# The first 512 rows' gated products moved into the rounds of the stage before, in a six-stage decoder kernel

## The reference

```python
x = _layernorm(x + _L0_attn_ref(x, ...))          # stage A: causal attention with a conv on v
x = _layernorm(x + _L0_xattn_ref(x, ctx_768, ...))  # stage B: cosine of Wv x and Wt ctx, 256 x 256, added to x
x = _layernorm(x + _L0_ffn_ref(x, ...))           # stage C: ternary feed-forward, below
x = _layernorm(x + _L1_attn_ref(x, ...))          # stage D: linear attention
x = _layernorm(x + _L1_xattn_ref(x, ctx_768, ...))  # stage E: cross attention
x = _layernorm(x + _L1_ffn_ref(x, ...))           # stage F: 8 experts, top 2
```

```python
def _L0_xattn_ref(visual_features, text_features, Wv, bv, Wt, bt):
    v = einsum('bsd,hd->bsh', visual_features, Wv) + bv
    t = einsum('bsd,hd->bsh', text_features, Wt) + bt
    dots = einsum('bih,bjh->bij', v, t)
    vn, tn = norm(v, axis=-1), norm(t, axis=-1)
    return dots / maximum(vn[:, :, None] * tn[:, None, :], EPS)
def _L0_ffn_ref(x, w1_w, w1_s, w2_w, w2_s, h1_w, h1_s, h2_w, h2_s, w3_w, w3_s):
    h = silu(_tlin(x, w1_w, w1_s)) * _tlin(x, w2_w, w2_s)   # 256 -> 1024, "gated products"
    h = gelu(_tlin(h, h1_w, h1_s))                          # 1024 -> 1024
    h = gelu(_tlin(h, h2_w, h2_s))
    return _tlin(h, w3_w, w3_s)                             # 1024 -> 256
```

## Time and profile before

| what | value |
|---|---|
| median of 3 runs | 1569.43 us (1557.24, 1571.11, 1569.43) |
| profiled execution, its own time | 1566.94 us |
| its span, first to last instruction | 1564.9 us |
| PE busy | 1326.4 us, 85% of the span |
| DVE, POOL, ACT busy | 1075.8, 800.9, 570.1 us |
| stages A and B, up to the last xt_lo | about 156.5 us |

### The profile page before, as it was taken

How to read it: one execution, slowest core, us unless ns; L and a number is a source line. 1 busy time by engine, 2 the same in 40 slices (tenths; PEclk the granted TensorE clock), 3 DMA queues, 4 the chain that set the end, 5 groups by cost and what they waited for, 6 DMA issues and landing times.

```text
span 1564.9 us, 23343 instructions
## 1 busy us (share of the span) xinstructions
PE 1326.4 (85%) x9071; PEld 1118.8 (71%) x9071; DVE 1075.8 (69%) x1729; ACT 570.1 (36%) x1171; POOL 800.9 (51%) x762
## 2 busy tenths in 40 slices
PE   6996999999989989977798989896582798989890
PEld 6985788778868868855566766665452798989890
DVE  4655766766676676543777677677673688888886
ACT  3666211211111021123344444443330565666552
POOL 4343666656656566523222433534443776767652
PEclk9997999999999999999999999998685899999995
DMA  5100333233223233212233215323400855555525
GB/s 167 37 21 1 111 94 115 81 92 98 81 81 99 76 94 94 61 39 56 94 99 120 82 40 120 88 58 95 115 8 25 293 211 192 209 191 207 192 71 161
DMA packets 58044, 163.23 MB, mean 104 GB/s; under 512 B 10598, under 2 KB 26185, under 8 KB 50000
## 3 DMA queue, kind: packets, MB, share of 16 engines
q1 hardware_dynamic: 45760, 100.13, 22.2%
q0 software_dynamic: 12176, 61.63, 11.1%
HBM read 136.47 MB, written 27.08 MB: 105 GB/s over the span
## 4 chain that ended last, share of the span: by engine, by line
PE 60%; DVE 17%; issue 7%; DMA 6%; ACT 5%; SPq 3%; POOL 2%; ACTq 0%; POOLq 0%; DVEq 0%
PE bank L388 13%; PE bank L390 13%; PE bank L389 13%; PE bank L1210 9%; PE bank L396 4%; SPq L717 3%; DVE topE L1714 2%; DVE hid_hi L1589 2%; DMA split_qk<-qk_lo 2%; PE bank L1052 2%; DVE shiftE L1723 2%; DMA xt_hi<-split_qk 2%; DVE hf L1605 2%; PE bank L1039 1%; PE bank L1128 1%
## 5 line engine op out<-in xcount | busy, mean ns | idle before, releaser
L520 POOL TENSOR_TENSOR wpiece_lo<-wraw,wpiece_hi 128x1024 fp32r<-128x1024 f32 x88 | 216.9, 2464 | 7.4
L1591 DVE TENSOR_TENSOR hid_lo<-hf,hid_hi 128x512 fp32r<-128x512 f32 x96 | 213.8, 2227 | 3.3
L388 PE MATMUL bank<-hid_hi,wpiece_lo 128*128 128x512 f32 x512 | 202.4, 395 | 12.9 <-DVE hid_lo L1591 12.9
L390 PE MATMUL bank<-hid_hi,wpiece_hi 128*128 128x512 f32 x512 | 200.7, 392 | 0.0
L389 PE MATMUL bank<-hid_lo,wpiece_hi 128*128 128x512 f32 x512 | 200.7, 392 | 0.0
L518 POOL TENSOR_SCALAR wpiece_hi<-wraw 128x1024 fp32r<-128x1024 f32 x88 | 95.0, 1080 | 186.2 <-PE bank L390 182.3
L1589 DVE CAST hid_hi<-hf 128x512 fp32r<-128x512 f32 x96 | 79.6, 830 | 125.7 <-ACT hf L1326 124.6
L1326 ACT ACTIVATE hf<-bank,ffn_scales 128x512 f32<-128x512 f32 x64 | 44.2, 690 | 293.8 <-PE bank L390 293.8
L636 POOL TENSOR_SCALAR staging<-staging 128x1024 f32<-128x1024 f32 x64 | 66.7, 1041 | 138.9 <-ACT staging L1411 138.6
L1210 PE MATMUL bank<-w_hi,gh_lo 128*128 128x256 f32 x368 | 106.1, 288 | 22.5 <-issue 21.8
L388 PEld LDWEIGHTS bank<-hid_hi,wpiece_lo 128*128 128x128 f32 x512 | 96.8, 189 | 39.1 <-DVE hid_lo L1591 19.3
(11 more groups left out here) (337 smaller groups left out, 3711.4 us busy)
## 6 DMA issues: line engine op xcount, KB each, us to landing
wraw<-in_C_w SPq DMA_DIRECT2D x88, 512.0 KB, 3.6
split_qk<-qk_hi SPq DMA_DIRECT2D x64, 128.0 KB, 2.4
split_qk<-qk_lo SPq DMA_DIRECT2D x64, 128.0 KB, 2.4
xt_lo<-split_qk SPq DMA_DIRECT2D x8, 1024.0 KB, 5.5
xt_hi<-split_qk SPq DMA_DIRECT2D x8, 1024.0 KB, 6.9
yc<-y_rows SPq DMA_DIRECT2D x16, 256.0 KB, 6.2
ctx_raw<-in_ctxT SPq DMA_DIRECT2D x16, 192.0 KB, 3.7
xraw<-in_xT SPq DMA_DIRECT2D x8, 256.0 KB, 3.5
```

What stands on the lines that cost most here:

```text
L388: pe.e.matmul(o, sl, mh, start=start and i == 0, stop=False)
L390: made = pe.e.matmul(o, sh, mh, start=False, stop=stop and i == n - 1)
L520: pool.e.tensor_tensor(pair[1], raw, f(pair[0]), ALU.subtract).then_inc(done, 1)
L1591: dve.e.tensor_tensor(lo[:, o, :], hf[o % 2][:, :], f(hi[:, o, :]), ALU.subtract).then_inc(s_hid, 1)
```

## The change

1. `ab_steps` gets eight steps G(0) to G(7), one for each hidden tile of the first block's gated products, in rounds 13 to 20, each last in its round (priority 6), and four steps PC(1) to PC(4), which split weight pieces 1 to 4 on POOL, in rounds 12, 14, 16 and 18 (priority 5). The products, the Silu, the multiplication and the split of these eight tiles are done there and left out of stage C's block 0.
2. PE no longer waits for all of stage B before them, only for sequences 0 and 1, which make the first 512 rows.
3. SP loads the scales in round 4 and no longer waits for stage B's end before it loads pieces 3 and on; POOL's wait there is gone too.
4. The buffers of stages A and B and of stage C are ordered so that `wpiece`, `hf`, `sg` and the scales overlap nothing of A and B, and `hid` overlaps only what is no longer in use when it is written.
5. The banks are dealt out in the new order.

```diff
+GPIECE = 5
 def ab_steps():
     items += [(6 + b, 0, "B", (b,), 7) for b in range(B)]
+    items += [(12 + 2 * (m - 1), 5, "PC", (m,), 1) for m in range(1, GPIECE)]
+    items += [(13 + o, 6, "G", (o,), 1) for o in range(FC)]
     return in_rounds(items)
...
 def bank_order():
     for name, step, args in AB:
         out += [((name, k, *args), every) for k in takes.get((name, step), "")]
+        if name == "G":
+            out += [(("C", "g", 0, *args, mat), every) for mat in range(2)]
     for s in range(NSB):
-        for n in range(4):
-            out += [(("C", "g", s, 2 * n + oo, mat), every) for oo in range(2) for mat in range(2)]
+        if s:
+            out += [(("C", "g", s, o, mat), every) for o in range(FC) for mat in range(2)]
...
 pool_program:
+                elif name == "PC":
+                    piece(*args)
...
-            wait_xt(pool, "B", B - 1)
             for s in range(NSB):
                 for n in range(NPIECE):
-                    if s or n:
+                    if s or n >= GPIECE:
                         piece(s * NPIECE + n)
...
 sync_program:
                 elif name == "P0":
+                    load(scl[:, :, :], a["C_s"], l_ffn)
+                    load(s3b[:, :], a["C_s3"], l_ffn)
                     for m in range(3):
                         piece(m)
...
-            wait_xt(sp, "B", B - 1)
-            load(scl[:, :, :], a["C_s"], l_ffn)
-            load(s3b[:, :], a["C_s3"], l_ffn)
             for m in range(3, NSB * NPIECE):
                 piece(m)
...
 tensor_program:
+            def gate(s, o):
+                wh, wl = wpiece[(s * NPIECE + o // 2) % 3]
+                pe.wait_ge(s_piece, s * NPIECE + o // 2 + 1)
+                for mat in range(2):
+                    u = use["C", "g", s, o, mat]
+                    terms = []
+                    for k in range(KC):
+                        c0 = ((mat * 2 + o % 2) * KC + k) * P
+                        terms.append(((wh[:, c0:c0 + P], wl[:, c0:c0 + P]),
+                                      (xt_hi[:, k, s * SB:(s + 1) * SB], xt_lo[:, k, s * SB:(s + 1) * SB])))
+                    pe.wait_ge(u.drained, u.turn)
+                    product(pe, u.ap[:, :], terms).then_inc(u.filled, 1)
...
+                elif name == "G":
+                    for b in range(BPS):
+                        wait_xt(pe, "B", b)
+                    gate(0, *args)
...
 scalar_program:
+            def gate(s, o):
+                u = use["C", "g", s, o, 0]
+                act.wait_ge(l_ffn, 32)
+                act.wait_ge(u.filled, u.full)
+                if o >= 2 or s:
+                    old = use["C", "g", *divmod(s * FC + o - 2, FC), 1]
+                    act.wait_ge(old.drained, old.done)
+                act.e.activation(sg[o % 2][:, :], u.ap[:, :], ACT.Silu, scale=scl[:, 0, o:o + 1]).then_inc(u.drained, 1)
...
+                elif name == "G":
+                    gate(0, *args)
...
 vector_program:
+            def gate(s, o):
+                gated, up = use["C", "g", s, o, 0], use["C", "g", s, o, 1]
+                dve.wait_ge(l_ffn, 32)
+                dve.wait_ge(up.filled, up.full)
+                dve.wait_ge(gated.drained, gated.done)
+                dve.e.scalar_tensor_tensor(out=hf[o % 2][:, :], in0=up.ap[:, :], scalar=scl[:, 1, o:o + 1], in1=sg[o % 2][:, :],
+                                           op0=ALU.mult, op1=ALU.mult).then_inc(up.drained, 1)
+                into_hidden(s, 0, o, up)
...
+                elif name == "G":
+                    gate(0, *args)
```

More of the change, by code:

```diff
@@ L272, in build @@
         ndiag_a = ring(2, lambda i: sb(f"ndiagA{i}", [P, TT, P], F32, early))
[L273 to L279, removed]
+        wraw = ring(3, lambda i: sb(f"wraw{i}", [P, CW], F32, late, "right"))
+        wpiece = ring(3, lambda i: hilo(f"wpiece{i}", [P, CW], late, "right"))
+        hf = ring(2, lambda i: sb(f"hf{i}", [P, SB], F32, late, "right"))
+        sg = ring(2, lambda i: sb(f"sg{i}", [P, SB], F32, late, "right"))
+        scl = sb("ffn_scales", [P, 4, FC], F32, late, "right")
+        s3b = sb("ffn_s3", [P, D], F32, late, "right")
         early.close()
@@ L927, in tensor_program @@
                         ln_pe(pe, "B", b)
+                elif name == "G":
+                    for b in range(BPS):
+                        wait_xt(pe, "B", b)
+                    gate(0, *args)
             for s in range(NSB):
-                cols = slice(s * SB, (s + 1) * SB)
                 seqs = range(s * BPS, (s + 1) * BPS)
[L932 to L940, removed]
-                            terms = []
-                            for k in range(KC):
-                                c0 = ((mat * 2 + oo) * KC + k) * P
-                                terms.append(((wh[:, c0:c0 + P], wl[:, c0:c0 + P]), x_in[k]))
-                            pe.wait_ge(u.drained, u.turn)
-                            product(pe, u.ap[:, :], terms).then_inc(u.filled, 1)
+                if s:
+                    for b in seqs:
+                        wait_xt(pe, "B", b)
+                    for o in range(FC):
+                        gate(s, o)
                 for layer in range(2):
@@ L1306, in scalar_program @@
                         ln_hi(act, "B", b, xt_part(xt_hi, b))
+                elif name == "G":
+                    gate(0, *args)
             for s in range(NSB):
-                act.wait_ge(l_ffn, 32)
-                for n in range(4):
-                    for b in range((s - 1) * BPS, s * BPS) if s and n == 0 else ():
+                if s:
+                    for b in range((s - 1) * BPS, s * BPS):
                         ln_apply(act, "C", b, resid[b % 3])
-                    for oo in range(2):
-                        o = 2 * n + oo
-                        u = use["C", "g", s, o, 0]
-                        act.wait_ge(u.filled, u.full)
-                        if o >= 2 or s:
-                            old = use["C", "g", *divmod(s * FC + o - 2, FC), 1]
-                            act.wait_ge(old.drained, old.done)
-                        act.e.activation(sg[o % 2][:, :], u.ap[:, :], ACT.Silu, scale=scl[:, 0, o:o + 1]).then_inc(u.drained, 1)
+                    for o in range(FC):
+                        gate(s, o)
                 for layer in range(2):
@@ L1488, in w_split, with into_hidden @@
                 dve.e.tensor_tensor(pair[1], raw, f(pair[0]), ALU.subtract).then_inc(done, 1)
+            def into_hidden(s, part, o, done):
+                hi, lo = hid[part % 2]
+                if part == 1:
+                    old = use["C", "h", s - 1, 1, FC - 1] if s else None
+                elif part == 2:
+                    old = use["C", "h", s, 0, FC - 1]
+                else:
+                    old = use["C", "y", s * BPS - 1] if s else None
+                if old:
+                    dve.wait_ge(old.filled, old.full)
+                dve.wait_ge(done.drained, done.done)
+                dve.mark(dve.e.tensor_copy(hi[:, o, :], hf[o % 2][:, :]))
+                dve.wait_own()
+                dve.e.tensor_tensor(lo[:, o, :], hf[o % 2][:, :], f(hi[:, o, :]), ALU.subtract).then_inc(s_hid, 1)
+            def gate(s, o):
[6 more added lines that the diff above has]
+                into_hidden(s, 0, o, up)
             for name, step, args in AB:
```

44 lines of the change are left out of this document (11 added, 33 removed).

## The result

| | before | after |
|---|---|---|
| median of 21 runs | 1569.43 us (1557.24 to 1590.89) | 1580.30 us (1569.95 to 1588.83) |
| ratio after to before, 95% interval | | 1.0066 [1.0043, 1.009] |
| profiled execution, its own time | 1566.94 us | 1574.61 us |
| its span | 1564.9 us | 1572.7 us |
| PE busy | 1326.4 us | 1346.8 us |

The surprise is in the row on PE: with the same matmuls it is busy 20 us longer, though the change could only spare it idle time. Part of this is scatter between executions (two more of the kernel after have 1338.9 and 1338.1 us, one more of the kernel before 1333.7). The stretches further down say where the rest lies. First the part that the forecast was about.

What follows compares the result with a forecast made beforehand. PE was taken to bound most stages, a mostly DVE ring the last rounds of stage B. 152.91 + 8.1 + 3.0 + 5.0 = 169.0, taken as 168.5; gain 174.15 - 168.5 = 5.7; 1566.94 - 5.7 = 1561.2, median 1562, range 1549 to 1574.

Steps and rivals of the forecast that it cites:

- The hole, and what bounds it: Last rounds of stage B: PE works 1.12 of 6 us, held by a mostly DVE ring of 5.53 us a round.
- DVE's tile, +1.62 a round: Stage B, rounds 13 to 17: a tile costs DVE at least 1.84 against 0.22 idle, 8.1 us in all.
- Round 13, x_tok(3) at 134.7: Stage B: first tile held by Silu's start and POOL's split; x_tok(3) at 134.7 against 130.05, +4.65, 3.0 beyond the 1.62.
- The pieces, 0.6 and twice 2.2: Stage B: POOL's splits PC(2), PC(3), PC(4) hold DVE's shift by 0.6, 2.2 and 2.2, sum 5.0 us.
- PE and ACT in the rounds at 0: Stage B rounds: G steps on PE and Silu on ACT have slack, cost 0; 4.5 if the clock stayed at half.
- X = 168.5: Stage B: start of x_tok of sequence 7, 152.91 before, taken as 168.5; the gain is 174.15 - X, 5.7 us.
- Rival B: Stage B: POOL and PE hold DVE in each tile as in stage C; x_tok(7) at 176.2, 2.1 us slower, 1569.0; chance 0.15.
- rival A: Stage B: POOL hardly touches the ring; x_tok(7) at 162.0, gain 12.1 us, 1554.8; chance 0.22.
- G(6) and G(7): End of stage B: after x_tok(7) only T(7), 0.77, and two G steps, 7.24, remain; second hidden tile at 183, not 188.5.
- The new SBUF addresses change no operation: Whole kernel: the new buffer layout was listed among the edits priced at nothing, 0 us.
- I carry it to the end in full: Stage C's block 0 and all after: they start from semaphores alone, so the 5.7 us gain lasts to the end.
- Rival C: Stage C's first layer: DVE or the pieces late all the same, so the move is worth nothing, 1567; chance 0.08.

Runs made afterwards that it cites:

- experiment 2: Kernel before with an unused buffer of 1152 bytes per partition ahead of `hid`, no step moved; ratio 1.0049 [1.0015, 1.0083], 1580.24 us.

## Why the prediction was wrong

By its own steps:

- **The hole, and what bounds it: right.** PE fills most of it, at a clock of 0.98 from 148 to 154.
- **DVE's tile, +1.62 a round: right.** Rounds without a piece take 7.18, before 5.53: +1.65. The shift starts straight behind xt_lo, without the 0.22.
- **Round 13, x_tok(3) at 134.7: right.** 135.95, less the 1.5 by which this execution entered stage B later, is 134.4. The addition into resid was held by PC(1), 1.40 for 0.69, and hid_lo by the context's split, 1.65 for 0.69. The forecast's 128.45 was misread in its rows: that is where the first xt_hi ends, the two end at 128.98. In the run Silu(0) stood behind one xt_hi and ahead of the other, so the start came out right.
- **The pieces, 0.6 and twice 2.2: right in size**, 0.25, 2.2 and 2.2 by the intervals (7.43, 9.40 and 9.35 against 7.18); 2.3 when round 16 was freed of its piece. One detail was not foreseen: hid_lo carries 0.7 of it beside the hi part, the shift 1.6.
- **Square after Silu at 0: right,** no load between them. PE and ACT in the rounds at 0: right; PE waited 5.90 for x_tok(7) before T(7).
- **X = 168.5: right.** x_tok(7) comes 60.8 after x_tok(0), so on the clock of before at 167.8. Rival B had 176.2, rival A 162.0.
- **G(6) and G(7): right.** From T(7), 170.46, to the first hidden matmul, 178.25, is 7.8; forecast 8.0. The second tile began at 183.8, on before's clock 182.3, forecast 183, with no wait for hid_lo.
- **"The new SBUF addresses change no operation": wrong, and this is the step that failed.** It stood among the edits at nothing, with no row behind it. It costs 8.7 us in blocks 0 to 3 of stage C, and experiment 2 has it without any moved step.
- **"I carry it to the end in full": wrong for the same reason.** The gain was there at 184 us and gone by the end of the hidden layers. Rival C had the gain taken back behind the moved point, but by a late piece; nothing waited. A later stage that takes over 1 us more was named as a sign that the forecast is wrong; stage C is that.

The sum with the missing term is -4.9 + 8.7 = +3.8 us, 0.24%. The profiled pair adds up column by column: 1.5 (entry) - 6.2 + 12.5 + 0.6 - 0.6 = +7.8, and 12.5 is more than 8.7 because the trace of before has the shortest h63-h0 of all, at a granted clock of 0.99 in that stretch against 0.98 in the trace of after. Of the change's three comparisons with before, 1.0022 and 1.0004 agree with +0.24%, and 1.0066 [1.0043, 1.009] lies above it by 0.2% at the least. These 3 us or more have no row: no trace of the changed kernel in the other sets shows them, and they stay open. That the median fell above the range of 1549 to 1574 rests on both, the missed 8.7 and this remainder: 1569.4 + 3.8 alone would be 1573.2, inside it. The range had no term for the one edit that touches all of stage C.

## What to carry to other kernels

When buffers are laid out anew, list each matmul operand's start address before and after, counted from one origin for all of them, with the number of matmuls that read it: a few ns on 1536 of them outweighed a well-judged 5 us, and 128 unused bytes bring them back. Read two kernels by the stride of the same instructions in a stretch where PE is full (here 174 against 178 matmuls in 40 us), since a gain ahead of it hides the loss in the end time. A step moved into an in-order ring is cheapest where its engine already waits (DVE's 1.88 before `recB`), not at the end of the round, where the next release stands behind it.

## What the runs showed of the hardware

- **The start of the operand with the 512 columns.** At full clock a matmul on `hid` follows the last after 227 ns on the mean with remainders 0, 256, 512, 1024 and 1280 bytes from the right edge, and after 232.4 to 233.4 with 64 and 1152. Counted from byte 0, the 227 ns come where `hid` starts at the same remainder by 256 as `wpiece` (224), and all four other places seen (`hid` at 96 and 160, `xt_hi` at 192 and 128) are at 232 to 234. `wpiece` was never moved, so the runs don't tell whether the remainder itself counts or the distance between the two operands. The last product has it the other way round: `wpiece` gives its 256 columns, and `hid` is the operand of 128. There the mean stride is 119.8 to 119.9 ns with `hid` on a line and 116.9 to 119.4 off it, so it does not share the loss.
- **POOL and DVE.** Beside a split on POOL, whole operations of DVE were held until POOL's instruction ended: the shift 1.73 for 0.15, hid_lo 1.40 for 0.69, the addition 1.40 for 0.69, and also the cast, which reads one buffer only, 2.04 for 0.43. Those with an input in PSUM (hf, xt_lo, recB) kept 0.68 to 0.75.
- **One stage differs from one set of runs to the next.** The kernel before had medians of 1552 to 1586 us in the sets of this study, and nearly all of that lies in stage F, the experts. From F to the end one set has 358 to 359 us in three kernels and 350 in the fourth, another 340 to 348, two others 326 to 327 in all seven, with the order of the steps and the address making no difference, while h63-h0 and F-h63 don't follow the set. Two of the sets bear the same chip number, and they have 340 to 348 and 326 to 327, so if that number names one chip, it is not the chip alone; what it is, no run tells. So times of different sets are not compared here, only ratios.
